# Deformable convolution on one core: sampling four centre rows at a time from eight pixel rows

## The chip, the cores and the metric

The kernel runs on one core of a Trainium2 chip. The metric is the device time of one execution in microseconds. The kernel before took 4288.97 us (median of 3 runs, 4286.38 to 4290.77).

## The reference

The input `x` is four images of 128 channels by 128x128 pixels, fp32. Two blocks follow one another, each with a residual: a deformable 3x3 convolution and a two-expert mixture; then a mixing step in the frequency domain and a pooled 64-expert network. Only the first part is touched by the change:

```python
offset = offset_conv(layernorm(x), w_off)        # 3x3, 18 outputs: (dy, dx) for each of 9 taps
py = base_y + ky + dy;  px = base_x + kx + dx     # a fractional place for every pixel and tap
sampled = bilinear_gather(layernorm(x), py, px)   # 4 corners, weights wy*wx
out = einsum('bckhw,ock->bohw', sampled, w_conv)  # then x + out
```

Each of the nine taps of each pixel reads the image at its own fractional place, which lies within two pixels of the regular one.

## The kernel before

The first stage is `phase_a`. It goes through the images in groups of four image rows (`NG` = 128 groups, 32 for each image), and in it "centre rows" `c` = -1 to 128: everything that a tap samples for a place on row `c` is computed once and then used by the three output rows c-1, c and c+1. An image has 130 centre rows (`NCB`).

**Sampling as matrix products.** For a strip of neighbouring pixels the bilinear weights are "hats": max(0, 1-|d|) in y times the same in x, over NJ pixel rows and NI pixel columns. The hats of a row (`a_hh`) are made on POOL, ACT and DVE, multiplied out by DVE for even centre rows and by POOL for odd ones (`prod`, L446 and L488) into 9 taps of NI x NJ values a pixel, and turned by DVE in 32x32 squares (`turn_s`, L456), so that the NI x NJ values lie on partitions (`a_tt`). The pixels themselves (`xtp`, a padded and normalised copy of the image in HBM, 128 channels = 512 bytes a pixel) are fetched as "windows" (`a_win`): NI columns by NJ rows of pixels, for each of NWIN strips in each of the four quarters (32 columns) of a row. Before, NI = 10, NJ = 6, and a strip serves NU_ = 6 places. The 60 pixels are split into two halves of 30 partitions, which are accumulated. One `sample` (L306 to L324) is half a pair of centre rows: 3 strips x 2 halves x 4 quarters = 24 products of a 30x128 stationary tile by 108 moving columns (6 centre and tap rows x 3 taps x 6 places). The four quarters stand on partitions 0, 32, 64 and 96, and each writes its own PSUM bank of `a_sb`. In fp32 the profile has each product as two records, so a block of a `sample` has 48.

**What follows a block.** ACT copies the bank contents into `a_sr`, a ring of 12 rows (L390 to L410), three copies for a block, or 12 smaller ones where the four rows go over the ring's end. `a_sb` is there once: the next block waits for these copies (`sr_ready`). When all rows of a group are there, `out` (L326 to L336) makes the output: 9 products of 128x128 weights by 512 columns, 18 records, into one bank (`a_ob`). DVE adds `x` (`residual`, L463), and SP stores it.

**The order** is written out by hand in `order_a` (L142 to L211). A step is a group of 4 centre rows (12 slots; 6 rows and 18 slots at an image's end). Every engine goes through the same list and takes its own entries. In step s PE does the four blocks of the pairs of group s at slots 0, 3, 6 and 9, the transposes, offset products and shifts of groups s+4 and s+2 between them, and the 9 output products of group s-1 at slots 7 to 17. `Once` (L24) leaves out a wait that has been met already.

**The fetches** are all issued by SP in the order of the list: `load` of x, `window` (L557 to L571) and the stores. Pair p's window is 16 DMAs of 30 KB (4 pixel rows by 4 quarters; 24 at the top of an image), each with a destination of 6 strips by 10 partitions of 512 bytes. The buffer is there twice (`NWB` = 2), so window p waits until pair p-2 is sampled.

## Time and profile before

| | |
|---|---|
| median of the runs | 4288.97 us |
| the profiled execution's own time | 4291.22 us |
| its span | 4289.4 us |
| PE busy, of the span | 4007.8 us (93%) |
| DVE, ACT, POOL busy | 2578.2, 1851.2, 1521.5 us |
| granted TensorE clock, mean | 0.949 |
| DMA packets | 726454, 757.45 MB |

The profile page says for each engine how long it was busy, then for each group of instructions its line, its shapes, its count and its mean duration. `a_` names belong to `phase_a`, `b_` to `d_` names to the later stages. The first stage lies from 0 to about 2263 us. "PEld" is TensorE's weight load, listed apart from the products. A granted clock of 1.00 is 2.4 GHz, one of 0.50 is 1.2 GHz. A product's duration in a row is longer than its distance to the next one, because products overlap in the engine; start times are what to compare.

### The profile page before, as it was taken

What the parts mean: (1) busy time and instruction counts of PE and PEld (TensorE: products, weight loads), DVE (VectorE), ACT (ScalarE), POOL (GpSimd) and SP (SyncE); (2) the same over time, 40 slices, a digit from 0 to 9 for tenths busy, and PEclk for the clock granted to TensorE, in tenths of its full rate; (3) what the DMA queues carried; (4) which work ended last, traced back from release to release, by engine and by line L of the source; (5) the groups of instructions that cost most, each with busy time, mean ns of one, the idle gap of its engine ahead of it and who ended that gap; (6) DMA issues with size and microseconds to landing.
All of it is one profiled execution on the core that took longest, in us unless ns stands there. A gap on an engine that the chain in (4) does not pass through costs nothing. (4 is left out here: it accounts for less than half of the span.)

```text
span 4289.4 us, 104769 instructions
## 1 busy us (share of the span) xinstructions
PE 4007.8 (93%) x37907; PEld 2583.6 (60%) x37907; DVE 2578.2 (60%) x8765; ACT 1851.2 (43%) x5607; POOL 1521.5 (35%) x2857
## 2 busy tenths in 40 slices
PE   5999999999999999999996999999999999997458
PEld 4666666666666666666663555666666666665245
DVE  3444434444343444344435888999999999977533
ACT  3555545555555555555540111333333333347124
POOL 3444444444444444444432222233323333245210
PEclk7999999999999999999997999999999999989655
DMA  3433333333333433334324666777777777744869
GB/s 121 113 107 109 112 103 113 107 110 111 109 107 108 113 107 109 106 109 113 107 86 169 245 246 245 262 258 259 265 268 258 259 259 264 261 161 133 332 246 395
DMA packets 726454, 757.45 MB, mean 177 GB/s; under 512 B 86176, under 2 KB 608928, under 8 KB 709552
## 3 DMA queue, kind: packets, MB, share of 16 engines
q1 hardware_dynamic: 620464, 676.79, 47.6%
q10 hardware_dynamic: 104448, 71.85, 5.2%
q8 instruction: 301, 4.93, 0.5%
q14 instruction: 217, 1.78, 0.1%
q0 software_dynamic: 1024, 2.10, 0.1%
HBM read 569.81 MB, written 179.54 MB: 175 GB/s over the span
## 5 line engine op out<-in xcount | busy, mean ns | idle before, releaser
L333 PE MATMUL a_ob<-a_sr,wcv 128*128 128x512 f32 x2304 | 1116.2, 603 | 0.8 <-DVE a_xo L463 0.8
L408 ACT COPY a_sr<-a_sb 128x384 f32<-128x384 f32 (+12 forms) x2346 | 691.4, 403 | 948.1 <-PE a_sb L322 948.1
L322 PEld LDWEIGHTS a_sb<-a_tt,a_win 30*128 30x128 f32 x24960 | 752.7, 188 | 410.3 <-issue 376.6
L322 PE MATMUL a_sb<-a_tt,a_win 30*128 30x108 f32 x24960 | 846.3, 278 | 22.3 <-DMA a_win<-xtp 20.8
L488 POOL TENSOR_TENSOR a_sx<-a_hh 128x540 f32<-128x540 f32 x260 | 358.8, 1380 | 794.9 <-DVE a_hh L438 767.2
L1044 DVE TENSOR_TENSOR b_P<-b_P,b_x 128x1024 f32<-128x1024 f32 x512 | 620.6, 1213 | 0.1
L333 PEld LDWEIGHTS a_ob<-a_sr,wcv 128*128 128x128 f32 x2304 | 396.3, 191 | 268.3 <-issue 251.2
L954 PE MATMUL b_z<-b_P,b_ew 128*128 128x512 f32 x1024 | 486.7, 619 | 0.0
L957 PE MATMUL b_z<-b_P,b_ew 128*128 128x512 f32 x1024 | 460.3, 592 | 0.0
L1175 POOL TENSOR_TENSOR b_ss<-b_st 128x12 f32<-128x12 f32 (+2 forms) x167 | 35.4, 212 | 1125.0 <-DVE b_pp L1119 994.6
L456 DVE STREAM_TRANSPOSE a_tt<-a_sx 128x576 f32<-128x576 f32 x520 | 403.1, 776 | 40.1 <-POOL a_sx L488 23.5
L463 DVE TENSOR_TENSOR a_xo<-a_ob,a_xin 128x512 f32<-128x512 f32 x128 | 88.6, 692 | 530.8 <-PE a_ob L333 530.8
L423 DVE BATCH_NORM_STATS2 a_st<-a_tk 128x6 f32<-128x128 f32 x512 | 114.1, 286 | 368.1 <-PE a_tk L285 368.1
L957 PEld LDWEIGHTS b_z<-b_P,b_ew 128*128 128x128 f32 x1024 | 194.6, 190 | 206.2 <-issue 201.5
L1191 POOL TENSOR_TENSOR b_rs<-b_ss,mhalf 128x12 f32<-128x12 f32 (+2 forms) x167 | 312.6, 1872 | 13.1 <-POOL b_ss L1187 0.2
L1017 ACT ACTIVATE c_tn<-c_x,b_rs 128x128 f32<-128x128 f32 x512 | 164.3, 393 | 347.6 <-POOL b_rs L1191 347.6
L954 PEld LDWEIGHTS b_z<-b_P,b_ew 128*128 128x128 f32 x1024 | 188.6, 194 | 207.5 <-issue 192.2
L438 DVE TENSOR_SCALAR a_hh<-a_hh 128x576 f32<-128x576 f32 (+1 forms) x128 | 59.5, 465 | 388.1 <-ACT a_hh L389 388.1
L346 ACT ACTIVATE a_tn<-a_tk,a_rs 128x128 f32<-128x128 f32 x512 | 213.3, 485 | 12.7 <-POOL a_rs L480 12.7
L446 DVE TENSOR_TENSOR a_sx<-a_hh 128x540 f32<-128x540 f32 x260 | 185.3, 713 | 4.5
L1388 PE MATMUL d_b<-ident,e_x 128*128 128x128 f32 x512 | 138.6, 426 | 45.1 <-DMA e_x<-x3d 43.3
L936 PE MATMUL b_rd<-b_iw,b_x 128*128 128x136 f32 x1024 | 154.8, 295 | 5.5 <-DVE b_lr L1069 3.5
(181 smaller groups left out, 5426.4 us busy)
## 6 DMA issues: line engine op xcount, KB each, us to landing
b_P<-pd SPq DMA_DIRECT2D x128, 2048.0 KB, 7.4
a_win<-xtp SPq DMA_DIRECT2D x4224, 30.0 KB
a_xin<-in_x SPq DMA_DIRECT2D x128, 256.0 KB, 3.1
xtp<-a_tn ACTq DMA_DIRECT2D x128, 256.0 KB, 3.4
x1d<-a_xo SPq DMA_DIRECT2D x128, 256.0 KB, 3.3
b_x<-x1d SPq DMA_DIRECT2D x128, 256.0 KB, 7.7
x2d<-b_xa SPq DMA_DIRECT2D x128, 256.0 KB, 2.8
d_wb<-in_w SPq DMA_DIRECT2D x16, 2048.0 KB, 19.3
```

What stands on the lines that cost most here:

```text
L322: t = e.matmul(d[:, :, :, NU_ * i:NU_ * i + NU_], win[32 * q:32 * q + NE, p % NWB, NWIN // 2 * h + i, j, :], m, start=(j == 0), stop=(j == 1))
L333: t = e.matmul(OB[:, :].rearrange("p (r x) -> p r x", r=4), k["wcv"][:, 3 * (2 - kr) + kx, :], rows[:, :, t_, :], start=(t_ == 0), stop=(t ...
L346: a = e.activation(tn[:, G % NTN, r, :], TK[:, r, :], ACT.Identity, bias=rs[:, G % 2, r:r + 1], scale=rs[:, G % 2, 4 + r:5 + r])
L408: a = e.copy(bass.AP(d.tensor, d.offset, [list(d.ap[0]), [1152, ni], [1536, nk], [32, 4], [1, m]]), bass.AP(v.tensor, v.offset, [list(v.ap ...
L446: e.tensor_tensor(sx[:, n % NST, :, 0:NI * NJ].rearrange("p t (j i) -> p t j i", j=NJ), hh[:, G % 2, i, :, None, 0:NI].to_broadcast([128, ...
L456: e.transpose(tt[:, p % NTP, 0:1152].rearrange("p (j a t x) -> p a t j x", j=2, a=2, t=9)[:, n % 2], bass.AP(v.tensor, v.offset, [list(v.a ...
L488: e.tensor_tensor(sx[:, n % NST, :, 0:NI * NJ].rearrange("p t (j i) -> p t j i", j=NJ), hh[:, G % 2, i, :, None, 0:NI].to_broadcast([128, ...
L954: e.matmul(ZE[u][:, :, :], ew[:, x, :], P[:, G % NPB, :, x, :], start=False, stop=False)
L957: t = e.matmul(ZE[u][:, :, :], ew[:, x, :], P[:, G % NPB, :, x, :], start=False, stop=(x == 7))
L1017: f = e.activation(tn3[:, u, r, :], x3t[:, G % 3, r, :], ACT.Copy, scale=rs[:, (G + LAG) % 2, 8 + r:9 + r])
L1044: t = e.tensor_tensor(v, v, x1[:, G % NX1, r, None, :].to_broadcast([128, 8, 128]), ALU.mult)
L1191: e.tensor_tensor(rs[:, u, c], ss[:, u, 2, c], k["mhalf"][:, c], ALU.pow).then_inc(scaled, 1)
```

## The change

Four centre rows ("a quad") are sampled together. NI = 8 and NJ = 8, so 64 pixels in two halves of 32 partitions; a strip serves NU_ = 4 places and there are NWIN = 9 strips. A quad takes three blocks (h = 0, 1, 2) of 3 strips x 2 halves x 4 quarters = 24 products of a 32x128 tile by 144 columns, at slots 0, 4 and 8 of the step. The two centre rows left over at an image's end are a quad of their own with 72 columns (slots 12, 14 and 16). The window of a quad is 8 pixel rows by 4 quarters, 32 DMAs of 36 KB (24 for the small quad), with 9 strips by 8 partitions of 512 bytes; it waits until quad Q-2 is sampled. `a_sr` has two rows more than its ring of 12, and the ring begins two rows earlier, so that ACT's copies never wrap: three a block. Where an output group goes over the ring's end, its products are split by rows into two (6 of 9 in every third group). The output products of group s-1 are made in step s+1, in slots 1 to 11; the work on group s+4 is put three slots earlier. `a_tt` is there for 3 quads in place of 4 pairs, and the ring of x has 10 places in place of 9.

```diff
@@ -94,12 +94,11 @@
 
 NCB = H + 2
 NCEN = B * NCB
-NPAIR = NCEN // 2
-NI, NJ = 10, 6
-NU_, NWIN = 6, 6
-NE = NI * NJ // 2
-NX, NTN, NYR, NOC = 9, 3, 12, 32
-NST, NTP, NWB, NSR = 2, 4, 2, 12
+NQUAD = B * (GI + 1)
+NI, NJ = 8, 8
+NU_, NWIN = 4, 9
+NX, NTN, NYR, NOC = 10, 3, 12, 32
+NST, NTP, NWB, NSR = 2, 3, 2, 12
 REACH = 2.0
 
...
@@ -122,6 +121,16 @@
 def products(n, odd):
 
     return n // 2 if odd else (n + 1) // 2
+
+
+def quad(Q):
+
+    b, q = divmod(Q, GI + 1)
+    return b * NCB + 4 * q, 4 if q < GI else 2
+
+
+def quad_of(n):
+    return n // NCB * (GI + 1) + n % NCB // 4
...
+    for s in range(-4, NG + 3):
         cs = chunk(s) if 0 <= s < NG else range(0)
         steps[s] = t0
-        for i, n in enumerate(cs):
-            samples[t0 + 3 * i] = n
+        for h in range(3 if len(cs) else 0):
+            samples[t0 + 4 * h] = (quad_of(cs[0]), h)
+            if len(cs) > 4:
+                samples[t0 + 12 + 2 * h] = (quad_of(cs[4]), h)
         t0 += max(3 * len(cs), 12)
     end = t0
-    for s in range(-4, NG + 2):
+    for s in range(-4, NG + 3):
         t0 = steps[s]
...
         if 0 <= F < NG:
-            put(t0, "turn", F)
-            put(t0 + 2, "stats", F)
-            put(t0 + 4, "scale", F)
-            put(t0 + 7, "conv", F, 0)
-            put(t0 + 10, "conv", F, 1)
-            put(t0 + 7, "norm", F, 0)
-            put(t0 + 8, "norm", F, 1)
-            put(t0 + 9, "norm_out", F)
-            put(t0 + 9, "y_out", F, 0)
-            put(t0 + 11, "y_out", F, 1)
+            put(t0 - 3, "turn", F)
+            put(t0 - 1, "stats", F)
+            put(t0 + 1, "scale", F)
+            put(t0 + 4, "conv", F, 0)
+            put(t0 + 8, "conv", F, 1)
+            put(t0 + 4, "norm", F, 0)
+            put(t0 + 5, "norm", F, 1)
+            put(t0 + 6, "norm_out", F)
+            put(t0 + 6, "y_out", F, 0)
+            put(t0 + 10, "y_out", F, 1)
...
             put(t0 + 9, "clip", Z)
-        if 0 <= s - 1 < NG:
-            for t, slot in enumerate((7, 8, 10, 11, 13, 14, 15, 16, 17)):
-                put(t0 + slot, "out", s - 1, t)
-            put(t0 + 18, "residual", s - 1)
-            put(t0 + 19, "x1_out", s - 1)
+        if 0 <= s - 2 < NG:
+            for t, slot in enumerate((1, 2, 3, 5, 6, 7, 9, 10, 11)):
+                put(t0 + slot, "out", s - 2, t)
+            put(t0 + 12, "residual", s - 2)
+            put(t0 + 13, "x1_out", s - 2)
     out = []
     windows = 0
     for slot in range(-12, end + 20):
         if slot in samples:
-            n = samples[slot]
-            while n % 2 == 0 and windows < min(n // 2 + NWB, NPAIR):
+            Q, h = samples[slot]
+            while h == 0 and windows < min(Q + NWB, NQUAD):
                 out.append(("window", windows))
                 windows += 1
-            out.append(("sample", n))
+            out.append(("sample", Q, h))
         out += at.get(slot, ())
     return out
...
@@ -223,9 +234,9 @@
     oc = S("a_oc", [128, NOC * 18 + 36])
     hh = S("a_hh", [128, 2, 6, 9, NI + NJ])
     sx = S("a_sx", [128, NST, 9, 64])
-    tt = S("a_tt", [128, NTP, 1154])
+    tt = S("a_tt", [128, NTP, 2306])
     win = S("a_win", [128, NWB, NWIN, 2, 128])
-    sr = S("a_sr", [128, NSR * 1152 + 1536])
+    sr = S("a_sr", [128, (NSR + 2) * 1152])
     xo = S("a_xo", [128, 2, 512])
     P = lambda name, shape: ctx.enter_context(nc.psum_tensor(name, shape, F32))
     TK = P("a_tk", [128, 4, 128])
...
@@ -306,32 +318,37 @@
             elif o[0] == "sample":
 
 
-                p, h = divmod(o[1], 2)
-                w.wait_ge(win_in[p % NWB], win_count[p])
+                _, Q, h = o
+                m_ = quad(Q)[1]
+                w.wait_ge(win_in[Q % NWB], win_count[Q])
                 w.wait_ge(filled, 1)
-                w.wait_ge(turned_s, 2 * p + 2)
-                w.wait_ge(sr_ready, 2 * p + h)
-                for i in range(NWIN // 2):
+                w.wait_ge(turned_s, quad(Q)[0] + m_)
+                w.wait_ge(sr_ready, 3 * Q + h)
+                for i in range(NWIN // 3):
                     for j in range(2):
                         for q in range(4):
-                            u = NU_ * (NWIN // 2 * h + i)
-                            m = tt[32 * q:32 * q + NE, p % NTP, 576 * j + u:576 * j + u + 1]
-
-                            m = bass.AP(m.tensor, m.offset, [list(m.ap[0]), [96, 6], [31, 3], [1, NU_]])
-                            d = SB[:, q, 0:324].rearrange("p (k t x) -> p k t x", k=6, t=3)
-                            t = e.matmul(d[:, :, :, NU_ * i:NU_ * i + NU_],
-                                         win[32 * q:32 * q + NE, p % NWB, NWIN // 2 * h + i, j, :], m,
+                            u = NU_ * (NWIN // 3 * h + i)
+                            m = tt[32 * q:32 * q + 32, Q % NTP, 1152 * j + u:1152 * j + u + 1]
+
+                            m = bass.AP(m.tensor, m.offset, [list(m.ap[0]), [96, 3 * m_], [31, 3], [1, NU_]])
+                            d = SB[:, q, 0:432].rearrange("p (k t x) -> p k t x", k=12, t=3)
+                            t = e.matmul(d[:, 0:3 * m_, :, NU_ * i:NU_ * i + NU_],
+                                         win[32 * q:32 * q + 32, Q % NWB, NWIN // 3 * h + i, j, :], m,
                                          start=(j == 0), stop=(j == 1))
                 t.then_inc(sampled, 1)
             elif o[0] == "out":
                 _, G, t_ = o
                 w.wait_ge(x1_ready, G)
-                w.wait_ge(sr_ready, last_centre(G) + 1)
+                w.wait_ge(sr_ready, 3 * quad_of(last_centre(G)) + 3)
                 kr, kx = divmod(t_, 3)
-                a = 4 * G % NSR * 1152
-                rows = sr[:, a:a + 4 * 1152].rearrange("p (r t x) -> p r t x", r=4, t=9)
-                t = e.matmul(OB[:, :].rearrange("p (r x) -> p r x", r=4), k["wcv"][:, 3 * (2 - kr) + kx, :],
-                             rows[:, :, t_, :], start=(t_ == 0), stop=(t_ == 8))
+                a = (4 * G - 2) % NSR
+                ob = OB[:, :].rearrange("p (r x) -> p r x", r=4)
+
+                m = 4 if a + 4 <= NSR else 2 + kr
+                for y, r, m in [(a, 0, m)] + ([(a + m - NSR, m, 4 - m)] if m < 4 else []):
+                    rows = sr[:, y * 1152:(y + m) * 1152].rearrange("p (r t x) -> p r t x", r=m, t=9)
+                    t = e.matmul(ob[:, r:r + m, :], k["wcv"][:, 3 * (2 - kr) + kx, :], rows[:, :, t_, :],
+                                 start=(t_ == 0 and r == 0), stop=(t_ == 8))
                 if t_ == 8:
                     t.then_inc(conv_out, 1)
 
...
@@ -388,32 +405,34 @@
                 w.wait_ge(hats_ready, G + 1)
                 e.activation(v, v, ACT.Abs).then_inc(bent, 1)
             elif o[0] == "sample":
-                p, h = divmod(o[1], 2)
-                b, c = centre(2 * p)
+                _, Q, h = o
+                n, m_ = quad(Q)
+                b, c = centre(n)
                 R = b * H + c - 1
-                w.wait_ge(sampled, 2 * p + h + 1)
-                w.wait_ge(conv_out, (min(R + 3, b * H + H - 1) - NSR) // 4 + 1)
-
-                if 0 <= c - 1 and c + 2 < H and R % NSR + 4 <= NSR:
-                    parts = [(0, 2, 0, 3)]
+                w.wait_ge(sampled, 3 * Q + h + 1)
+                w.wait_ge(conv_out, (min(R + m_ + 1, b * H + H - 1) - NSR) // 4 + 1)
+
+                if c < 0:
+                    parts = [(0, 1, 2, 1), (1, 1, 1, 2), (2, 2, 0, 3)]
+                elif m_ < 4:
+                    parts = [(0, 1, 0, 2), (1, 1, 0, 1)]
                 else:
-                    parts = [(i, 1, first - R - i, m) for i in range(2) for first, _, m in
-                             runs(R + i + tap_rows(2 * p + i)[0],
-                                  tap_rows(2 * p + i)[1] - tap_rows(2 * p + i)[0], NSR)]
+                    parts = [(0, 4, 0, 3)]
                 for kx in range(3):
-                    x, m = (18 - kx, 14 + kx) if h else (0, 18 - kx)
+                    x = max(0, 12 * h - kx)
+                    m = min(31, 12 * h + 11 - kx) + 1 - x
                     for i, ni, kr, nk in parts:
-                        d = sr[:, (R + i + kr) % NSR * 1152 + kr * 384 + kx * 128 + x:][:, 0:1]
-                        v = SB[:, 0, (9 * i + 3 * kr + kx) * 18 + (0 if h else kx):][:, 0:1]
+                        d = sr[:, ((R - 2) % NSR + i + kr) * 1152 + kr * 384 + kx * 128 + x:][:, 0:1]
+                        v = SB[:, 0, (9 * i + 3 * kr + kx) * 12 + x + kx - 12 * h:][:, 0:1]
                         a = e.copy(bass.AP(d.tensor, d.offset, [list(d.ap[0]), [1152, ni], [1536, nk], [32, 4], [1, m]]),
-                                   bass.AP(v.tensor, v.offset, [list(v.ap[0]), [162, ni], [54, nk], [512, 4], [1, m]]))
+                                   bass.AP(v.tensor, v.offset, [list(v.ap[0]), [108, ni], [36, nk], [512, 4], [1, m]]))
                 a.then_inc(sr_ready, 1)
 
     def vector(e):
         w = Once(e)
         e.memset(oc[:, :], 0.0)
         e.memset(sx[:, :, :, :], 0.0)
-        e.memset(tt[:, :, 1152:1154], 0.0).then_inc(filled, 1)
+        e.memset(tt[:, :, 2304:2306], 0.0).then_inc(filled, 1)
         for o in order:
             if o[0] == "stats":
                 G = o[1]
...
-                w.wait_ge(sampled, 2 * (p - NTP) + 2)
-                v = sx[:, n % NST, :, 0:1]
-                e.transpose(tt[:, p % NTP, 0:1152].rearrange("p (j a t x) -> p a t j x", j=2, a=2, t=9)[:, n % 2],
-                            bass.AP(v.tensor, v.offset, [list(v.ap[0]), [64, 9], [NE, 2], [1, 32]])
-                            ).then_inc(turned_s, 1)
+                w.wait_ge(sampled, 3 * (Q - NTP) + 3)
+                e.transpose(tt[:, Q % NTP, 0:2304].rearrange("p (j a t x) -> p a t j x", j=2, a=4, t=9)[:, n - quad(Q)[0]],
+                            sx[:, n % NST, :, :].rearrange("p t (j x) -> p t j x", j=2)).then_inc(turned_s, 1)
             elif o[0] == "residual":
                 G = o[1]
                 w.wait_ge(conv_out, G + 1)
...
@@ -555,20 +572,20 @@
                 e.dma_start(xin[:, G % NX, :],
                             ins["x"][b * 128:(b + 1) * 128, 4 * q * W:4 * q * W + 512]).then_inc(x_in[G % NX], 16)
             elif o[0] == "window":
-                p = o[1]
-                b, c = centre(2 * p)
-                last = b * GI + min(GI - 1, (c + 3) // 4)
-                w.wait_ge(tn_out[last % NTN], 16 * (last // NTN + 1))
-                if last % GI:
-                    w.wait_ge(tn_out[(last - 1) % NTN], 16 * ((last - 1) // NTN + 1))
-                w.wait_ge(sampled, 2 * (p - NWB) + 2)
-                for y in win_rows[p]:
-                    i = (y + 6) % 6
+                Q = o[1]
+                n, m_ = quad(Q)
+                b, c = centre(n)
+                last = b * GI + min(GI - 1, (c + m_ + 1) // 4)
+                for g in range(max(b * GI, last - 2), last + 1):
+                    w.wait_ge(tn_out[g % NTN], 16 * (g // NTN + 1))
+                w.wait_ge(sampled, 3 * (Q - NWB) + 3)
+                for y in win_rows[Q]:
+                    i = (y + 8) % 8
                     for q in range(4):
                         src = bass.AP(xtp.tensor, (b * PIX + (y + 3) * PC + 32 * q) * 128,
                                       [[128, NI], [NU_ * 128, NWIN], [1, 128]])
-                        d = 32 * q + NI * (i % 3)
-                        e.dma_start(win[d:d + NI, p % NWB, :, i // 3, :], src).then_inc(win_in[p % NWB], 16)
+                        d = 32 * q + NI * (i % 4)
+                        e.dma_start(win[d:d + NI, Q % NWB, :, i // 4, :], src).then_inc(win_in[Q % NWB], 16)
             elif o[0] == "x1_out":
                 G = o[1]
                 b, q = divmod(G, GI)
...
@@ -1658,9 +1675,10 @@
     x, t, i = np.arange(128)[:, None, None], np.arange(9)[None, :, None], np.arange(NI)[None, None, :]
     cx = ((x % 32 + t % 3) % NU_ + 2 - i).astype(np.float32)
 
-    m, j = np.arange(12)[:, None], np.arange(NJ)[None, :]
-    cy = np.where(m % 2 == 1, (m - j + 3) % 6 - 3, (m - j + 2) % 6 - 2).astype(np.float32)
-    cy = np.broadcast_to(cy[None], (128, 12, NJ))
+    m, j = np.arange(14)[:, None], np.arange(NJ)[None, :]
+    a = 5 - (m + 1) % 4
+    cy = ((m - j + a) % 8 - a).astype(np.float32)
+    cy = np.broadcast_to(cy[None], (128, 14, NJ))
     base = (np.arange(128)[:, None] // 64 + 2 * np.arange(2)[None, :]).astype(np.float32) * (H * W)
     far = np.zeros((128, 9, 2), np.float32)
```

## Rows read from the trace of the kernel before

**Rows 1.** Window in the sampling stage: PE, PEld, DVE, ACT, POOL busy; clock; DMA.
```profile
214.00:321.00 107.00, 107.00 (x1434) 69.71 (x1434) 44.29 (x120) 59.14 (x197) 46.85 (x78) 1.00 0.39 107
```
**Rows 2.** Groups by line and form, 0 to 2280 us: busy us, mean ns; idle before.
```profile
L446 DVE TENSOR_TENSOR a_sx<-a_hh 128x540 f32<-128x540 f32 x260 | 185.3, 713 | 4.5
L488 POOL TENSOR_TENSOR a_sx<-a_hh 128x540 f32<-128x540 f32 x260 | 358.8, 1380 | 794.9 <-DVE a_hh L438 767.2 <-DVE a_tt L456 27.7
L408 ACT COPY a_sr<-a_sb 128x432 f32<-128x432 f32 x211 | 110.5, 524 | 489.2 <-PE a_sb L322 489.2
L408 ACT COPY a_sr<-a_sb 128x336 f32<-128x336 f32 x211 | 93.6, 443 | 287.1 <-PE a_sb L322 287.1
```
**Rows 3.** Timeline of PE, one inner step: start, us, line, operation, records.
```profile
534.12 1.02 PE L333 MATMUL a_ob<-a_sr,wcv 128*128 128x512 f32 x2
534.98 0.78 PE L303 MATMUL a_yo<-a_zz,shift 128*128 128x72 f32 x6
535.60 1.07 PE L333 MATMUL a_ob<-a_sr,wcv 128*128 128x512 f32 x2
536.60 1.60 PE L322 MATMUL a_sb<-a_tt,a_win 30*128 30x108 f32 x48
538.13 2.84 PE L333 MATMUL a_ob<-a_sr,wcv 128*128 128x512 f32 x6
540.91 1.61 PE L322 MATMUL a_sb<-a_tt,a_win 30*128 30x108 f32 x48
542.44 0.82 PE L294 MATMUL a_yb<-wof,a_xin 128*128 128x162 f32 x4
543.10 1.88 PE L333 MATMUL a_ob<-a_sr,wcv 128*128 128x512 f32 x4
...
553.43 1.60 PE L322 MATMUL a_sb<-a_tt,a_win 30*128 30x108 f32 x48
```
**Rows 4.** Timeline of ACT in that step: the copies behind one block.
```profile
542.58 1.31 ACT L408 COPY a_sr<-a_sb 128x432 f32<-128x432 f32 x3 [3.12 <-PE a_sb L322]
```
**Rows 5.** Timeline of SP, start of the kernel and an inner step.
```profile
77.30 12.14 SPq L571 DMA_DIRECT2D a_win<-xtp  x32
...
529.79 14.47 SPq L571 DMA_DIRECT2D a_win<-xtp  x32
544.31 0.36 SPq L555 DMA_DIRECT2D a_xin<-in_x  x1
544.71 0.43 SPq L576 DMA_DIRECT2D x1d<-a_xo  x1
```
**Rows 6.** Waits of the SP queue over the kernel: us, times, longest.
```profile
SPq L571 <- PE a_sb L322: 248.0, 127, 10.2
SPq L33 <- PE a_sb L322: 139.0, 114, 3.5
```
**Rows 7.** DMA from 100 to 2200 us: a queue's packets, MB, share; issues.
```profile
q1 hardware_dynamic: 315959, 186.97, 31.8%
q10 hardware_dynamic: 82128, 36.53, 6.1%
...
a_win<-xtp SPq DMA_DIRECT2D x4018, 30.0 KB
```
**Rows 8.** Timeline of PE where one image ends.
```profile
608.59 1.60 PE L322 MATMUL a_sb<-a_tt,a_win 30*128 30x108 f32 x48 [1.36 <-DMA a_win<-xtp]
...
618.11 2.91 PE L322 MATMUL a_sb<-a_tt,a_win 30*128 30x108 f32 x48 [5.16 <-DMA a_win<-xtp]
620.95 1.45 PE L294 MATMUL a_yb<-wof,a_xin 128*128 128x162 f32 x4
```
**Rows 9.** Timeline of PE, the stage's first steps and its end.
```profile
58.47 2.91 PE L322 MATMUL a_sb<-a_tt,a_win 30*128 30x108 f32 x48
...
94.50 1.61 PE L322 MATMUL a_sb<-a_tt,a_win 30*128 30x108 f32 x48
...
2254.80 7.99 PE L333 MATMUL a_ob<-a_sr,wcv 128*128 128x512 f32 x18 [0.79 <-DVE a_xo L463]
```

More of the change, by code:

```diff
@@ L150, in order_a @@
     t0, samples, steps = 0, {}, {}
-    for s in range(-4, NG + 2):
+    for s in range(-4, NG + 3):
         cs = chunk(s) if 0 <= s < NG else range(0)
         steps[s] = t0
-        for i, n in enumerate(cs):
-            samples[t0 + 3 * i] = n
+        for h in range(3 if len(cs) else 0):
+            samples[t0 + 4 * h] = (quad_of(cs[0]), h)
+            if len(cs) > 4:
+                samples[t0 + 12 + 2 * h] = (quad_of(cs[4]), h)
         t0 += max(3 * len(cs), 12)
     end = t0
-    for s in range(-4, NG + 2):
+    for s in range(-4, NG + 3):
         t0 = steps[s]
@@ L264, in phase_a @@
     win_rows, win_count, total = {}, {}, [0] * NWB
-    for p in range(NPAIR):
-        c = centre(2 * p)[1]
-        win_rows[p] = range(c - 2, c + 4) if c < 3 else range(c, c + 4)
-        total[p % NWB] += 16 * 4 * len(win_rows[p])
-        win_count[p] = total[p % NWB]
+    for Q in range(NQUAD):
+        n, m = quad(Q)
+        c = centre(n)[1]
+        win_rows[Q] = range(c - 2, c + m + 2)
+        total[Q % NWB] += 16 * 4 * len(win_rows[Q])
+        win_count[Q] = total[Q % NWB]
     z_count, total = {}, 0
@@ L451, in vector @@
                 n = o[1]
-                p = n // 2
+                Q = quad_of(n)
                 w.wait_ge(weighed_pool if n % 2 else weighed_dve, n // 2 + 1)
-                w.wait_ge(sampled, 2 * (p - NTP) + 2)
-                v = sx[:, n % NST, :, 0:1]
-                e.transpose(tt[:, p % NTP, 0:1152].rearrange("p (j a t x) -> p a t j x", j=2, a=2, t=9)[:, n % 2],
-                            bass.AP(v.tensor, v.offset, [list(v.ap[0]), [64, 9], [NE, 2], [1, 32]])
-                            ).then_inc(turned_s, 1)
+                w.wait_ge(sampled, 3 * (Q - NTP) + 3)
+                e.transpose(tt[:, Q % NTP, 0:2304].rearrange("p (j a t x) -> p a t j x", j=2, a=4, t=9)[:, n - quad(Q)[0]],
+                            sx[:, n % NST, :, :].rearrange("p t (j x) -> p t j x", j=2)).then_inc(turned_s, 1)
             elif o[0] == "residual":
@@ L520, in gpsimd @@
                                     k["cx"][:, None, :, :].to_broadcast([128, m, 9, NI]), ALU.add)
-                    y = (centre(first)[1] + 6) % 6
+                    y = (centre(first)[1] + 8) % 8
                     a = e.tensor_tensor(hh[:, G % 2, i:i + m, :, NI:NI + NJ], v[:, :, :, 0:1].to_broadcast([128, m, 9, NJ]),
@@ L1632, in program @@
             k |= {"wof": SA("wof", [128, 162]), "shift": SA("shift", [128, 3, 128]), "wcv": SA("wcv", [128, 9, 128]),
-                  "cx": SA("cx", [128, 9, NI]), "cy": SA("cy", [128, 12, NJ])}
+                  "cx": SA("cx", [128, 9, NI]), "cy": SA("cy", [128, 14, NJ])}
             with ExitStack() as c0:
```

## The prediction

> **What bounds the kernel now.** I read the page first (which engine, where in the span), then the windows, the timeline of each engine over one step, and the waits. In the sampling stage TensorE is never idle in 107 us, at a granted clock of 1.00, which is 2.4 GHz; DVE is busy 44 us of 107, ACT 59, POOL 47 [rows 1]. So the stage takes what PE's list takes, and only what shortens that list, or makes PE wait, counts. An inner step runs from 536.60 to 553.43, 16.83 us [rows 3]. The reader is to compare starts in it, not durations:
>
> - Two output records of 512 columns take 534.98 - 534.12 = 0.86, so 0.43 each, or 0.84 ns a column.
> - Six records of 72 columns take 0.62, 0.103 each, where 0.84 ns a column would be 0.060. There is a floor of about 0.105 to 0.11 us under a record with a 128-column weight load. Four records of 162 columns take 0.66; less some 0.10 of leaving the block ahead, that is 0.14 each, and 162 x 0.84 = 0.136: above the floor the columns decide.
> - A sampling block (48 records) takes 1.53 (536.60 to 538.13). Its records run four abreast, in 12 rounds, so a round is at most 0.128, and 0.11 if 0.2 of the block is filling. That is the floor again: 108 columns would be 0.091. The block also costs 0.20 outside itself: six output records between two blocks take 2.78, not 2.58. One block is 1.73.
>
> SP is the second to look at. It issues 32 windows in 12.14 us when nothing is beside them (0.38 each), in 14.47 in an inner step, and 0.8 for the other two transfers [rows 5]. It waits for PE 387 us in 128 steps, 3 us a step [rows 6]. That slack is what the change has to fit into.
>
> **The change, part by part.**
>
> *Blocks.* Four blocks of a step become three. The columns stay (4 x 108 = 3 x 144), the weight loads and the edges fall by a quarter. A round now needs 144 x 0.84 = 0.121, over the floor. I take 0.123 for 0.111, so a block is 1.53 + 12 x 0.0125 = 1.68, with its edges 1.88. The price of a 144-column round has no row: from below it is 0.121; from above, the old round of at most 0.128 may hide up to 0.017 of something beside the 0.091 of columns (the moving operand is now read in runs of 4 elements, before of 6), which would make it about 0.141. I take the low value because the 72-, 162- and 512-column records all lie on floor or columns. Before: 520 blocks x 1.73 = 899.6. After: 384 x 1.88 + 12 small ones (72 columns, at the floor) x 1.73 = 742.7. **Gain 157 us**; with rounds of 0.141 it is 157 - 384 x 12 x 0.018 = 74 us.
>
> The Trainium skill (TensorE: Matmul & The Clock Gate, section on packing small matmuls, "The mechanism") says that a weight load overlaps products in flight only when its row group differs. By that a round of the block would be load plus columns, 0.107 + 0.091 = 0.198 before and 0.227 after, and the step would gain 12 x (4 x 0.198 - 3 x 0.227) = 1.3 us, no more than by my rows. The trace does not agree: 12 such rounds would be 2.4 us and the block takes 1.53.
>
> *Wrapped outputs.* In every third group 6 of 9 output products are cut in two: 43 x 6 x 2 = 516 more records. Their columns are the same and the smallest, 128 columns, is 0.1075, at the floor. 3 ns each, **2 us**; at most 516 x 0.02 = 10.
>
> *ACT's copies.* Three of 576, 528 and 480 elements (h = 0), 3 x 576 (h = 1), 384 to 480 (h = 2), where it was 432, 408 and 384. By the two forms (524 ns for 432, 443 for 336) an element costs 0.84 ns; three copies take 1.31 for 1224 elements [rows 2, 4], so 1.6, 1.75 and 1.4 us now. PE's cover before it needs `a_sb` again: after h = 0 the shift and three outputs, 0.62 + 2.6 = 3.2; after h = 1 and h = 2 an offset product, 0.55 + 2.6 = 3.1 and more. ACT must also get there in time: after h = 1 it has four `norm` activations, `y_out` and `bend` (about 3.3 us) before the copies of h = 2, while PE needs 5.0 from the end of h = 1 to the end of h = 2; it comes at 1.75 + 3.3 = 5.1, a tenth late, with 1.5 us of cover left. Cost nothing; if that cover went, each late us would cost 128.
>
> *DVE and POOL.* The products grow from 540 to 576 elements: 713 and 1380 ns [rows 2] become 760 and 1470, twice a step, beside PE. `residual` for one group now stands between the last output (slot 11) and the next first output (slot 13), with a block and the shift, 2.5 us, between; DVE needs 0.7 plus what is left of the statistics ahead of it. Before there was more air here. I cost it at nothing; up to 0.5 us a step (64 us) if `bend` and `clip` run late.
>
> *SP and the windows.* Still 32 issues a step, each 36 KB for 30. Window Q+1 can start when quad Q-1 is done (about slot 9.5 of the step before) and is needed at the step after: 1.2 steps, 18.6 us, against 12.2 + 0.8 and some 2 us of landing, my guess. Behind a waiting window on SP stand the next store and load; the store of x1 was done long before, and `load` is five groups ahead. If issue time follows the bytes it is 0.46, 14.6 + 0.8 = 15.4 a step: just under PE's new 15.55, and then the image ends and hiccups show. I cost it at nothing; the ends are 0 and 0.4 us a step (50 us).
>
> The Trainium skill (DMA: Bandwidth & Descriptors, "Why a DMA increments its semaphore by 16 and not by 1") gives the engines of such a transfer as the largest number up to 16 that divides its slowest dimension. That speaks against the change: 10 partitions went over 10 engines, 8 go over 8, with 9 packets each instead of 6. The trace agrees for the 10: 315,959 packets of q1 less about 242 large transfers of 144 leave 70 for each of 4018 windows, 60 of data and 10 that close [rows 7]. In load, q1's 31.8% of 16 engines is at most 51% of ten; times 1.5 and a step shorter by 1.08 it is 83%, 89% with q10: not full.
>
> *Image ends.* Before, PE waits 1.36 + 5.16 us for a window and then runs at half clock for a while (an offset pair 1.45 instead of 0.82, a block 2.91 for 1.60) [rows 8]: about 10 us, three times. Now the next image's first window starts when quad 31 is done and takes 12.2 + 2 us; PE has 0.6 + 2.6 + 0.5 of other work and three small blocks (5.2), between which it waits about 1.2 us twice for copies with nothing to cover them: 11.3, so a stall of 3, and less half clock. 8 us each. **Gain 6.**
>
> *Start and end.* One more output group is left for after the last block: 8 us for a group alone [rows 9]. At the start steps 0 and 1 took 58.47 to 94.50; they are bound by windows and by half clock, and step 1 loses its 7.7 us of outputs, of which I count 3 beyond the blocks already counted. **Loss 5.**
>
> Sum: 4291.2 - 157 + 2 - 6 + 5 = 4135 for the profiled execution's own time, which is 2.25 over the median of the runs; so 4133 for the median.
>
> **The rivals.**
>
> 1. *A dearer round.* 0.13 to 0.141 us: 4165 to 4216. For it: no row shows 144 columns or runs of four. Against: the other shapes fit to 0.003.
> 2. *SP or a late engine takes some of it.* The step is PE's 15.55 plus 0.2 to 0.5 (issue time by bytes, or `residual` late): 4160 to 4200. For: SP has 2.5 us left, half of which the trace already loses to disturbances (14.47 for 12.14). Against: a 256 KB issue takes 0.36 to 0.43 [rows 5], so size hardly matters.
> 3. *Windows become the bound, slower than before.* Place: SP's chain of 32 issues and the engines under it. It decides from (16.83 - 0.8) / 32 = 0.50 us an issue. If an issue's distance grew by half, to 0.57, as the packets of one engine do, a step would be 32 x 0.57 + 0.8 = 19.0: +2.2 us x 128, 4570. Against: the load above, and 0.38 looks like SP's own time.
> 4. *Nothing gained.* If the waits for `a_sb` (single, now with longer copies) or for rows ate 1.2 us a step, the time stays at 4289. It needs 1.5 us of cover and 1.2 more to go.
>
> **How the numbers follow.** My forecast has 0.70, rival 1 0.13, rival 2 0.10, rival 3 0.05, rival 4 0.02. The forecast's own range is 4115 to 4155 (the round 0.121 to 0.127, image ends 0 to 10 us each). With most of rivals 1 and 2 it is 4105 to 4205. A run of this kernel can tell 0.2%, 9 us, from no change. Faster by more: 0.70 + 0.13 + 0.10 = 0.93; slower 0.05; same 0.02.
>
> **What would show it.** An inner step of 15.5 to 15.6 us; a block of 1.68, and 0.20 around it; PE at 107 of 107 us; SP with 32 issues in 12 to 15 us and still waiting for PE; three copies of 1.6 to 1.75. I am wrong if PE waits for `a_win` in inner steps, if SP's waits for PE vanish, if the block is over 1.8, or if PE waits for `a_xo` before an output.

## The result, and the profile after

The changed kernel takes 4237.8 us (median of 4 runs, 4234.1 to 4238.6) against 4289.9 before (4 runs): a ratio of 0.9876, 95% interval 0.9859 to 0.9893. It is faster by 52 us. I had forecast 4133, with a range of 4105 to 4205: the direction was right, two thirds of the gain did not come.

First the whole span: 4235.3 us where it was 4289.4. The last output product of the first stage ends at 2214.4, before at 2262.8 [rows 9], so 48 of the 54 us lie in that stage. The later stages, which are the same code, took 2026.6 before and 2020.9 now; nothing in the change or in my forecast accounts for these 6 us.

One inner step on PE in the timeline of the changed kernel (start us, duration us, line, operation, records), which answers to [rows 3]:

```profile
532.48 1.88 PE L350 MATMUL a_ob<-a_sr,wcv 128*128 128x512 f32 x4
534.30 1.89 PE L335 MATMUL a_sb<-a_tt,a_win 32*128 32x144 f32 x48
536.11 0.89 PE L315 MATMUL a_yo<-a_zz,shift 128*128 128x72 f32 x6
536.84 2.80 PE L350 MATMUL a_ob<-a_sr,wcv 128*128 128x256 f32 x12
539.57 1.88 PE L335 MATMUL a_sb<-a_tt,a_win 32*128 32x144 f32 x48
541.38 0.82 PE L306 MATMUL a_yb<-wof,a_xin 128*128 128x162 f32 x4
...
544.73 1.88 PE L335 MATMUL a_sb<-a_tt,a_win 32*128 32x144 f32 x48
...
550.31 1.88 PE L335 MATMUL a_sb<-a_tt,a_win 32*128 32x144 f32 x48
```

The step is 550.31 - 534.30 = 16.01 us where I wanted 15.5 to 15.6, and a block is 536.11 - 534.30 = 1.81, not 1.68. ACT and SP are as foreseen. Three copies take 1.6 to 1.8 us (1.4 behind the third block), the 32 issues of a window take 12.8, and SP still waits 362 us for PE over the kernel (before 387 [rows 6]):

```profile
541.53 1.76 ACT L427 COPY a_sr<-a_sb 128x576 f32<-128x576 f32 x3 [3.56 <-PE a_sb L335]
```

```profile
546.67 12.81 SPq L588 DMA_DIRECT2D a_win<-xtp  x32
```

A step of 16.0 would still be 105 us less than 16.83 over 128 steps. The other loss is between the steps. Two stretches of the changed kernel (busy us of PE, PEld, DVE, ACT, POOL, then granted clock and DMA share) no longer show PE at 107 of 107 [rows 1], and the DMA share has gone from 0.39 to 0.65 for transfers of 36 KB in place of 30:

```profile
214.00:321.00 107.00, 106.06 (x1223) 72.16 (x1223) 44.32 (x113) 58.38 (x133) 49.86 (x73) 1.00 0.65 127
535.00:642.00 107.00, 97.62 (x1173) 68.99 (x1168) 40.25 (x100) 49.95 (x144) 45.21 (x69) 0.92 0.64 112
```

The waits, 0 to 2280 us (us, times, longest): PE stands 56 us for windows in 30 places, before 20.8 us in 7. Of the 56, 6.3 are at the start and 23.6 at the three image ends; the rest is spread over inner steps.

```profile
PE a_sb L335 <- DMA a_win<-xtp: 56.0, 30, 8.8
```

The DMA queue from 100 to 2100 us, beside [rows 7] (packets, MB, share of 16 engines):

```profile
q1 hardware_dynamic: 348123, 207.15, 56.5%
...
a_win<-xtp SPq DMA_DIRECT2D x3923, 36.0 KB
```

The share rose from 31.8% to 56.5%. Of all that q1 did, 0.565 x 16 x 2000 / 3923 = 4.6 us of DMA engine time fall on one transfer of a window; before 0.318 x 16 x 2100 / 4018 = 2.7. A fifth more bytes took 70% more engine time. In the trace's records of single packets the same shows directly: from 100 to 2100 us a 512-byte packet of q1 lasts 50 ns on average, before 28 ns (before, the median is 27). A "list" is the share of a transfer that one engine gets: 348,123 packets less about 238 large transfers of 144 leave 80 a transfer, 72 of data and 8 that close, so there are eight lists now, as the rule of the Trainium skill (DMA: Bandwidth & Descriptors, "Why a DMA increments its semaphore by 16 and not by 1") had it.

An image's end, beside [rows 8]: the wait is longer than before, 8.46 us (6.26 and 8.84 at the other two ends), and the block behind it takes 3.2 us in place of 1.8, at a granted clock of 0.50.

```profile
581.81 1.57 PE L335 MATMUL a_sb<-a_tt,a_win 32*128 32x72 f32 x48
584.31 1.83 PE L335 MATMUL a_sb<-a_tt,a_win 32*128 32x72 f32 x48 [0.92 <-ACT a_sr L427]
...
598.42 3.26 PE L335 MATMUL a_sb<-a_tt,a_win 32*128 32x144 f32 x48 [8.46 <-DMA a_win<-xtp]
```

So there were two questions: why a window takes so much more of the DMA engines, and why a block takes 1.81.

### The profile page after: what moved, and what is told of

Read it like the earlier page. It is cut to its first block and busy times, and to the rows that moved or that the text cites. A ratio compares the mean times of both kernels' runs of the same rounds, so it can differ in the third digit from the quotient of the medians.

```text
span 4235.3 us, 92558 instructions
## 1 busy us (share of the span) xinstructions
PE 3893.6 (92%) x32471; PEld 2584.2 (61%) x32471; DVE 2584.4 (61%) x8765; ACT 1774.3 (42%) x4557; POOL 1595.6 (38%) x2857
## 3 DMA queue, kind: packets, MB, share of 16 engines
q1 hardware_dynamic: 660144, 701.54, 60.2%
## 5 line engine op out<-in xcount | busy, mean ns | idle before, releaser
L350 PE MATMUL a_ob<-a_sr,wcv 128*128 128x512 f32 (+3 forms) x2820 | 1085.3, 519 | 0.8 <-DVE a_xo L480 0.8
L427 ACT COPY a_sr<-a_sb 128x576 f32<-128x576 f32 (+7 forms) x1296 | 621.0, 562 | 977.9 <-PE a_sb L335 970.1
L335 PEld LDWEIGHTS a_sb<-a_tt,a_win 32*128 32x128 f32 x19008 | 662.6, 187 | 315.5 <-issue 208.1
L335 PE MATMUL a_sb<-a_tt,a_win 32*128 32x144 f32 x19008 | 755.9, 302 | 67.7 <-DMA a_win<-xtp 56.0
L505 POOL TENSOR_TENSOR a_sx<-a_hh 128x576 f32<-128x576 f32 x260 | 378.9, 1457 | 930.6 <-DVE a_hh L457 922.5
L350 PEld LDWEIGHTS a_ob<-a_sr,wcv 128*128 128x128 f32 x2820 | 493.6, 192 | 280.4 <-issue 232.1
L971 PE MATMUL b_z<-b_P,b_ew 128*128 128x512 f32 x1024 | 476.7, 608 | 0.0
L974 PE MATMUL b_z<-b_P,b_ew 128*128 128x512 f32 x1024 | 460.3, 592 | 0.0
L363 ACT ACTIVATE a_tn<-a_tk,a_rs 128x128 f32<-128x128 f32 x512 | 196.1, 485 | 8.8 <-POOL a_rs L497 8.8
L465 DVE TENSOR_TENSOR a_sx<-a_hh 128x576 f32<-128x576 f32 x260 | 193.0, 742 | 4.4
L968 PE MATMUL b_z<-b_pT,b_ebm 32*128 32x128 f32 x1024 | 148.6, 284 | 0.0
```

Source lines behind the costliest of these rows:

```text
L335: t = e.matmul(d[:, 0:3 * m_, :, NU_ * i:NU_ * i + NU_], win[32 * q:32 * q + 32, Q % NWB, NWIN // 3 * h + i, j, :], m, start=(j == 0), sto ...
L350: t = e.matmul(ob[:, r:r + m, :], k["wcv"][:, 3 * (2 - kr) + kx, :], rows[:, :, t_, :], start=(t_ == 0 and r == 0), stop=(t_ == 8))
L363: a = e.activation(tn[:, G % NTN, r, :], TK[:, r, :], ACT.Identity, bias=rs[:, G % 2, r:r + 1], scale=rs[:, G % 2, 4 + r:5 + r])
L427: a = e.copy(bass.AP(d.tensor, d.offset, [list(d.ap[0]), [1152, ni], [1536, nk], [32, 4], [1, m]]), bass.AP(v.tensor, v.offset, [list(v.ap ...
L465: e.tensor_tensor(sx[:, n % NST, :, 0:NI * NJ].rearrange("p t (j i) -> p t j i", j=NJ), hh[:, G % 2, i, :, None, 0:NI].to_broadcast([128, ...
L505: e.tensor_tensor(sx[:, n % NST, :, 0:NI * NJ].rearrange("p t (j i) -> p t j i", j=NJ), hh[:, G % 2, i, :, None, 0:NI].to_broadcast([128, ...
```

## The experiments

### The windows

**w_spread**: the same 32 transfers in another order.

```diff
-                for y in win_rows[Q]:
-                    i = (y + 8) % 8
-                    for q in range(4):
+                for y, q in [(y, q) for q0 in (0, 1) for y in win_rows[Q] for q in (q0, q0 + 2)]:
+                    i = (y + 8) % 8
+                    if True:
```

> The changed kernel with the 32 window transfers of a quad issued in another order: quarters 0 and 2 of every pixel row first, then quarters 1 and 3 (before: quarters 0, 1, 2, 3 of one row, then the next row). Nothing else changes. In the changed kernel the fetch queue's packets take 60.2% of 16 engines' span where they took 47.6%, for 8% more packets. Theory A (transfers close behind one another write to partitions that are served together, and the order decides how they collide): the share falls towards 50%, PE's waits for a_win fall from 56 us to under 20, time about 4200. Theory B (eight transfer lists with 9 packets each are simply more work for each list): share and waits stay, time 4238 within 10. Theory C (the cost lies on the reading side, where each pixel is now fetched twice): as B.

Measured: 4184.4 us, 0.9765 of before (0.9748 to 0.9782), so 53 us less than the changed kernel from the order alone. The share of q1 from 100 to 2100 us is 47.5% for more transfers, a packet takes 40 ns, and PE's waits fall to 14.6 us in 4 places, one at the start and three at the image ends, none in an inner step:

```profile
q1 hardware_dynamic: 353948, 210.23, 47.5%
...
a_win<-xtp SPq DMA_DIRECT2D x3999, 36.0 KB
```

```profile
PE a_sb L335 <- DMA a_win<-xtp: 14.6, 4, 5.5
```

Only theory A had this: how transfers that follow one another disturb each other depends on their order. The order changes where they write in turn, and also what they read in turn; w_src8 below varies the reading.

**w_same**: the opposite order.

```diff
-                for y in win_rows[Q]:
-                    i = (y + 8) % 8
-                    for q in range(4):
+                for y, q in [(y, q) for y0 in range(4) for q0 in (0, 2) for q in (q0, q0 + 1)
+                             for y in win_rows[Q][y0::4]]:
+                    i = (y + 8) % 8
+                    if True:
```

> The changed kernel with the 32 window transfers of a quad in the worst order by theory A: four transfers that write to the same eight partitions of a quarter or of its neighbour follow one another (rows y and y+4, quarters 0 and 1; then the same for quarters 2 and 3). Spreading them cut the queue's packets from 60.2% to 55.9% and the time by 53 us. If what collides is transfers into partitions that are 0 or 32 apart, packets get longer still (over 70 ns on average), PE waits for a_win in most steps, and the time rises over 4300, perhaps to 4900. If only the distance between rows mattered, or the spread order won for another reason, it stays near 4238.

Measured in one run: 4432.6 us, 195 over the changed kernel and 146 over the kernel before run beside it (4286.3). The same bytes in the same transfers: PE waits 179 us up to 2350 us, in 55 places, which is less than every second step. The granted clock over the first stage is 0.94, where the changed kernel had 0.98.

```profile
PE a_sb L335 <- DMA a_win<-xtp: 179.2, 55, 8.8
```

```profile
1819.00:1926.00 107.00, 98.29 (x1128) 67.79 (x1124) 40.77 (x107) 52.42 (x142) 46.09 (x71) 0.94 0.67 120
```

The share of q1 is 59.2% for 3623 transfers, 5.2 us each against 3.8 in the spread order. Between the spread order and this one lie 248 us. The packets did not reach the 70 ns I gave (58), and with 50 ns most of the disturbance is there in the changed kernel's own order already. The Trainium skill (SBUF — State Buffer, "Door 1: The DMA port swizzle") has quarters 0 and 1 (partitions from 0 and from 32) on the same DMA ports, quarters 2 and 3 too, and quarters 64 partitions apart on different ones; the orders agree with it: 0 and 1 in a row are bad, 0 and 2 good. No run here varied the distance by itself, and w_same also puts transfers to the very same eight partitions behind one another. So the shared ports are what fits, not what was isolated.

**w_src8**: other source addresses.

```diff
-                        src = bass.AP(xtp.tensor, (b * PIX + (y + 3) * PC + 32 * q) * 128,
-                                      [[128, NI], [NU_ * 128, NWIN], [1, 128]])
+                        src = bass.AP(xtp.tensor, (b * PIX + (y + 3) * PC + 16 * q) * 128,
+                                      [[128, NI], [8 * 128, NWIN], [1, 128]])
```

> The changed kernel with other source addresses only: strips begin 8 pixels apart in place of 4, so no pixel is fetched twice by one transfer (quarters begin 16 pixels apart to stay in the row; what is fetched is not what the reference needs, the sampled values are wrong). Theory C: packets fall to the 27 ns they had before, q1's share under 50%. Theories A and B: share stays at about 60%.

Measured in one run: 4233.8 us (the changed kernel 4234.1 to 4238.6), q1 at 60.4% of the whole span (60.2% in the changed kernel), packets at 50 ns. That each pixel is read twice costs nothing that shows; theory C falls.

**w_six**: two thirds of the bytes.

```diff
-                                      [[128, NI], [NU_ * 128, NWIN], [1, 128]])
+                                      [[128, NI], [NU_ * 128, 6], [1, 128]])
...
-                        e.dma_start(win[d:d + NI, Q % NWB, :, i // 4, :], src).then_inc(win_in[Q % NWB], 16)
+                        e.dma_start(win[d:d + NI, Q % NWB, 0:6, i // 4, :], src).then_inc(win_in[Q % NWB], 16)
```

> The changed kernel fetching 6 of the 9 strips (24 KB a transfer; the strips left out are zeros, so part of the sampling is left out). Same number of transfers and products. Theory B: with 6 packets for each of 8 lists the load is that of before for each list; packets fall to 27 to 30 ns, waits for a_win under 15 us, time 4185 to 4200. Theory A: packets fall too, since each collision is shorter, but less, to 35 to 45 ns. If the time stays at 4238, the windows are not what is lost.

Measured: 4181.6 us (0.9755, 0.9739 to 0.9771); q1 27.8% from 100 to 2100 us, half of 56.5% for two thirds of the data:

```profile
q1 hardware_dynamic: 258229, 161.23, 27.8%
```

Packets are at 28 ns again, as theory B had it, in the order of the changed kernel and on the same eight lists. PE waits 10.0 us in three places, the image ends (2.9, 3.4 and 3.7). So it takes both: the order of the destinations, and enough packets in a list. With a transfer issued every 0.35 to 0.40 us, 9 packets a list are over that point and 6 are not. That the disturbance begins when a list is still at work as the next transfer comes would explain both runs; no run here shows it.

**w_halves**: each pixel row once for two quads. The buffer is a ring of four halves of four rows; in the constants, a hat's place moves by 3.

```diff
-    win = S("a_win", [128, NWB, NWIN, 2, 128])
+    win = S("a_win", [128, 2 * NWB, NWIN, 128])
...
+def half_rows(h):
+    b, g = divmod(h, GI + 2)
+    return b, range(4 * g - 3, min(4 * g + 1, H + 3))
...
+                                         win[32 * q:32 * q + 32, (hf + (hf + j) % 2) % (2 * NWB),
+                                             NWIN // 3 * h + i, :], m,
...
-    cy = ((m - j + a) % 8 - a).astype(np.float32)
+    cy = ((m - j + 3 + a) % 8 - a).astype(np.float32)
...
```

> The changed kernel, but the window buffer is a ring of four half windows of four pixel rows. A quad uses two neighbouring halves, so each pixel row is fetched once for two quads: 16 transfers of 36 KB a step in place of 32. Same sizes of transfer, same products, same order of the list. If the windows are what is lost beyond the inner step of 16.0 us (theories A, B and C alike), PE's waits for a_win go to nearly 0 except at the start, the image ends shrink, and the time is 4170 to 4195. If the waits only look like window waits and the loss is elsewhere (the list, the copies), it stays over 4220.

Measured: 4169.7 us (0.9730, 0.9714 to 0.9747). That is 68 us less than the changed kernel, with PE's waits for windows down to 2.6 us: the windows' whole price, half clock behind the waits included. It is 12 us more than w_six gives, which still waits at the image ends.

**w_both**: w_halves with the spread order.

```diff
-                for y in ys:
-                    i = (y + 3) % 4
-                    for q in range(4):
+                for y, q in [(y, q) for q0 in (0, 1) for y in ys for q in (q0, q0 + 2)]:
+                    i = (y + 3) % 4
+                    if True:
```

> The changed kernel with both cures: each pixel row fetched once for two quads (16 transfers a step) and the transfers spread over the quarters (0 and 2, then 1 and 3). Halving the transfers alone gave 4169.7 with packets still at 60 ns, as no wait was left for them to cause in inner steps. If only waits count: 4162 to 4172, packets under 45 ns. If slow packets also cost elsewhere (PE, the image ends, the start), under 4160.

Measured: 4171.3 us (0.9737, 0.9721 to 0.9753), the same as w_halves. Packets are shorter (37 ns for 60) and PE does not wait for a window at all, so it is worth nothing: slow packets cost only through PE's waits.

### The block

The 48 records of a block start in 12 rounds of four. In the traces the rounds of a block are 0.112 us apart before and 0.133 in the changed kernel.

**r_contig** and **r_psum**: the moving operand read side by side, and PSUM written side by side.

```diff
-                            m = bass.AP(m.tensor, m.offset, [list(m.ap[0]), [96, 3 * m_], [31, 3], [1, NU_]])
+                            m = bass.AP(m.tensor, m.offset, [list(m.ap[0]), [12, 3 * m_], [4, 3], [1, NU_]])
```

```diff
-                            t = e.matmul(d[:, 0:3 * m_, :, NU_ * i:NU_ * i + NU_],
+                            t = e.matmul(SB[:, q, 144 * i:144 * i + 36 * m_],
```

> The changed kernel, whose sampling products read 144 moving elements that lie side by side, in place of 36 runs of 4 (the values are then not the right hats; part of the sampling is wrong). A round of four products took 0.112 us before and 0.133 in the changed kernel, where 144 columns at 0.84 ns are 0.121. Theory A (short runs of the moving operand cost): round 0.121 to 0.123, block 1.69, inner step 15.6. Theory B (the cost is of columns, or of four products abreast): round stays at 0.133, block at 1.81, step at 15.98.

> The changed kernel, whose sampling products write 144 columns of PSUM side by side, in place of 36 runs of 4 (the copies then take the values from the wrong places). Theory A (short runs on the writing side cost): round 0.121 to 0.123, step 15.6. Theory B: round stays at 0.133.

Measured: the block of r_contig is 703.11 - 701.43 = 1.68, the very number of the forecast; that of r_psum stays at 704.32 - 702.50 = 1.82. The timelines of r_contig and then of r_psum:

```profile
701.43 1.75 PE L335 MATMUL a_sb<-a_tt,a_win 32*128 32x144 f32 x48
703.11 0.89 PE L315 MATMUL a_yo<-a_zz,shift 128*128 128x72 f32 x6
```

```profile
702.50 1.88 PE L334 MATMUL a_sb<-a_tt,a_win 32*128 32x144 f32 x48
704.32 0.89 PE L315 MATMUL a_yo<-a_zz,shift 128*128 128x72 f32 x6
```

It is the read of the moving operand; the rounds of r_contig are 0.122 us apart. (r_contig took 4203.6, r_psum 4240.1, one run each.)

**r_108**: three of four centre rows.

```diff
-                            m = bass.AP(m.tensor, m.offset, [list(m.ap[0]), [96, 3 * m_], [31, 3], [1, NU_]])
+                            m = bass.AP(m.tensor, m.offset, [list(m.ap[0]), [96, min(9, 3 * m_)], [31, 3], [1, NU_]])
```

> The changed kernel with 108 columns in a sampling product in place of 144: one of four centre rows is left out of the products (copies and outputs unchanged). If a round is columns plus a fixed 0.013 with a floor of 0.112: 0.112, block 1.53, step 15.98 - 3 x 0.28 = 15.1. If short runs are what costs, 27 runs of 4 would show: round about 0.115 or more.

Measured in one run: block 708.73 - 707.19 = 1.54, rounds 0.112 us apart, 4167.3 us. 108 columns lie on the floor of before, with runs of 4 as with runs of 6; whatever the runs cost there, 0.091 of columns hides it under the floor. This is why the trace of before could not show it.

```profile
707.19 1.61 PE L335 MATMUL a_sb<-a_tt,a_win 32*128 32x108 f32 x48
708.73 0.89 PE L315 MATMUL a_yo<-a_zz,shift 128*128 128x72 f32 x6
```

**r_align**: the same runs of 4, each at a multiple of 16 bytes.

```diff
-                            m = bass.AP(m.tensor, m.offset, [list(m.ap[0]), [96, 3 * m_], [31, 3], [1, NU_]])
+                            m = bass.AP(m.tensor, m.offset, [list(m.ap[0]), [100, 3 * m_], [32, 3], [1, NU_]])
...
+                e.transpose(bass.AP(d.tensor, d.offset, [list(d.ap[0]), [100, 3], [33, 3], [1200, 2], [1, 32]]),
```

> The changed kernel with another layout of the turned hats: each tap's 32 values begin 33 elements after the last tap's (groups of three begin 100 apart), so a product reads its 36 runs of 4 at offsets 100k + 32t + u, all multiples of 16 bytes; before 96k + 31t + u, two of three runs not. 144 elements side by side gave a round of 0.122 in place of 0.133. Theory A (runs that cross 16-byte borders cost): round 0.122 to 0.124, inner step 15.6, time about 4195 to 4205 (the window waits stay). Theory B (any run of 4 costs, aligned or not): round 0.133, time 4235 to 4245.

Measured: the block is 713.75 - 712.07 = 1.68, so theory A is right about the round. (The run changes the two strides with the borders, so another property of the strides 96 and 31 is not excluded.) The forecast of the time failed: 4248.5 us (five runs, 4241.0 to 4269.8; 0.9928, 0.9902 to 0.9954), where 4195 to 4205 was expected, and above the changed kernel. The profile is of the slowest of the five. In it PE waits 105.4 us for windows, where it was 56. The step is shorter, the windows are not, and a wait can cost again behind it:

```profile
703.62 1.97 PE L335 MATMUL a_sb<-a_tt,a_win 32*128 32x144 f32 x48 [2.75 <-DMA a_win<-xtp]
705.52 1.56 PE L315 MATMUL a_yo<-a_zz,shift 128*128 128x72 f32 x6
706.87 5.26 PE L350 MATMUL a_ob<-a_sr,wcv 128*128 128x256 f32 x12
712.07 1.75 PE L335 MATMUL a_sb<-a_tt,a_win 32*128 32x144 f32 x48
```

The outputs at 706.87 take 5.2 us instead of 2.7, at a granted clock of 0.52, behind 2.75 us of idleness (the same columns as in the stretches above):

```profile
706.87:712.07 5.20, 5.20 (x14) 3.81 (x14) 1.05 (x3) 0.50 (x2) 1.60 (x3) 0.52 0.64 66
```

Not every wait does this: behind the next one, of 1.19 us at 723.80, the block takes 1.68 and the clock stays. Over the stage the sum is what counts: it ends at 2246.4 here and at 2104.1 in best, which has the same blocks and no such waits. Of these 142 us 105 are waits, so up to 37 lie in slower products behind them.

**best**: w_both and r_align together.

> w_both and r_align together. By theory A of r_align: 4166 less 384 blocks x 12 x 0.011 = 51 us, so about 4115. By theory B: as w_both, 4162 to 4172. If SP, ACT or DVE is just behind PE at 15.98 us a step, it comes out between, with PE waiting for one of them in inner steps.

Measured: 4121.9 us (4121.6 to 4123.7), 0.9627 of before (0.9611 to 0.9643), 116 us less than the changed kernel. The step is 725.29 - 709.67 = 15.62 us, and in the stretch below PE is at 107 of 107 again.

```profile
709.67 1.75 PE L344 MATMUL a_sb<-a_tt,a_win 32*128 32x144 f32 x48
711.36 0.89 PE L322 MATMUL a_yo<-a_zz,shift 128*128 128x72 f32 x6
...
725.29 1.75 PE L344 MATMUL a_sb<-a_tt,a_win 32*128 32x144 f32 x48
```

```profile
214.00:321.00 107.00, 107.00 (x1252) 71.84 (x1254) 47.42 (x125) 57.82 (x134) 54.45 (x81) 1.00 0.37 92
```

### The later outputs

**b_late**: that part of the change alone, in the kernel before.

```diff
-        if 0 <= s - 1 < NG:
-            for t, slot in enumerate((7, 8, 10, 11, 13, 14, 15, 16, 17)):
-                put(t0 + slot, "out", s - 1, t)
+        if 0 <= s - 2 < NG:
+            for t, slot in enumerate((1, 2, 3, 4, 5, 7, 8, 10, 11)):
+                put(t0 + slot, "out", s - 2, t)
```

> The kernel before with one part of the change alone: output products of group s-1 one step later (step s+1, slots 1 to 11, the ring of x with 10 places). Pairs, windows and blocks stay. My prediction gave this part 8 us of outputs left after the last block, partly won back at the start: 4289 to 4297. If the later outputs opened a wait (for the ring of rows, or the sum with x between the last and the next first output), it would be over 4305.

Measured: 4285.5 us against 4283.3, ratio 1.0009 (0.9999 to 1.0019), 10 runs. That cannot be told from no change.

## Why the prediction was wrong

**Blocks, the gain of 157 us.** The count was right: three blocks for four. The size of a round was not. I chose 0.123 from bounds of 0.121 and 0.141; it was 0.133. I had named the runs of 4 as what might be hidden, and then took the low end because the other shapes fitted. None of those shapes was read in runs that start off a 16-byte border and bound by columns at once. Price: 384 x 0.13 = 50 us; best against w_both gives 49. Of the 0.46 us by which the step is over my 15.55, three blocks make 0.39; 0.07 a step, 9 us, also stand in best (15.62) and stay open.

**SP and the windows, costed at nothing.** This is the step that failed. The issues went as foreseen (12.8 us for 32), but I took the packets' 27 ns as given. They take 50 ns. I had reckoned the load at 83% of eight engines, all of q1 laid on them; the same sum now gives 56.5% x 2 = 113%. How much packets of one queue disturb one another depends on the order of their destinations and on how many a list holds (w_spread, w_six), and in the trace of before only 4% of them took more than 35 ns. My rival 3 looked for the point where the issues become the bound (0.50 us). What came was a middle: windows that are late in some steps, while SP goes on waiting for PE. w_six, which has the packets back at 28 ns, gives back 56 us, w_spread 53 with the order alone. Rival 2 had the size about right (25 to 60 us) and the cause wrong. Of my signs of being wrong two came: waits for `a_win` in inner steps, and a block over 1.8.

**The two add up.** 4133 + 50 + 56 = 4239, beside the 4237.8 measured. That this meets to 1 us is luck. The kernel before took 4289.9, 4288.3, 4286.3 and 4283.3 us in the four series that the runs come from, and by the ratios the two terms are 47 and 52 us; 6 us of the gain lie in later stages. The 68 us of w_halves are not the number to add, as they hold waits at the image ends that the forecast had counted. Each term alone would have ended at 4183 or 4189, inside the range; I had given them as alternatives and let the range end at 4205.

**Image ends.** I gave 8 us each with a wait of 3. With packets at 28 ns the waits are 2.9, 3.4 and 3.7 (w_six), so that sum held for quick packets; in the changed kernel they are 8.46, 6.26 and 8.84, so no gain of 6 was left. In best PE has no wait for windows there. **The start**: the first block came at 69.7 us, before at 58.47; it too waited for windows (6.3 us), and comes at 58.7 in w_spread. **Wrapped outputs, ACT, DVE, later outputs**: as predicted. Twelve cut records took 2.73 us (536.84 to 539.57) where six whole ones took 2.72 in the next step, and PE never waited for the sum with x in an inner step.

## What to carry to other kernels

When a change makes one engine's step shorter, price the supplier at its worst order as well as at its mean: here the order of 32 unchanged transfers was worth 53 us one way and 195 the other. A wait of TensorE can cost more than itself: 105 us of waits in r_align had up to 37 us of slower products behind them. So removing work in front of a late transfer can make a kernel slower (r_align alone). A price that is hidden under a floor in the trace is unknown, not zero; measure it before the floor is removed.

## What was not expected of the hardware

- Products of 144 fp32 columns read in 36 runs of 4 take 1.81 us a block when two of three runs start off a 16-byte border, and 1.68 when all lie on one or when the 144 lie side by side. The length of the runs costs nothing, their place does: 0.011 us for a round of four records, 9%. Writing PSUM in runs of 4 costs nothing (1.82 side by side).
- Small transfers to eight partitions run at 28 ns a packet of 512 bytes with 6 packets a list, and at 50 with 9, in one and the same order; spread over the quarters they take 40, in the order of w_same 58.
